# Graph attention on one core: v's first half ahead of the transposes in the prologue, the second spill of row terms moved back, the last maximum turned behind value steps and a second step held

## The reference

```python
h = jnp.maximum(_layernorm(x, axis=-1), 0.0)          # x: 4096 x 256, float32
q, k, v = h @ Wq.T + bq, h @ Wk.T + bk, h @ Wv.T + bv # 256 x 256 weights
a = q @ k.T / 16 + adj + adj                          # 4096 x 4096
x = x + softmax(a, axis=-1) @ v
```

## Time and profile before

| | us |
|---|---|
| median of 3 runs | 810.15 |
| the runs | 810.07, 810.15, 2887.47 |
| the profiled execution | 809.79 |
| its span, first to last instruction | 808.0 |
| TensorE busy in it | 799.6 |
| VectorE, GpSimd, ScalarE busy | 561.3, 412.7, 357.2 |

### The profile page before, as it was taken

One profiled execution on the slowest core, in us unless ns is written; L12 is line 12 of the kernel. 1 busy time (PEld: TensorE's weight loads), 2 busy tenths in 40 slices (PEclk: granted clock), 3 DMA queues, 4 the chain that ended last, 5 costly groups with the idle time before them and its releaser, 6 DMA issues.

```text
span 808.0 us, 16606 instructions
## 1 busy us (share of the span) xinstructions
PE 799.6 (99%) x6652; PEld 797.6 (99%) x6652; DVE 561.3 (69%) x942; ACT 357.2 (44%) x637; POOL 412.7 (51%) x377
## 2 busy tenths in 40 slices
PE   9999999999999999999999999999999999999998
PEld 8999999999999999999999999999999999999998
DVE  6868767676676767667677666767766676776754
ACT  5684434434443443444344444344444444443365
POOL 4545719073471917447091643709164380926573
PEclk9999999999999999999999999999999999999999
DMA  8520434333333334333333333423333343333300
GB/s 256 180 94 5 161 91 120 98 112 97 97 114 93 112 98 110 100 98 119 92 111 93 112 105 91 123 92 106 101 111 106 83 123 91 110 105 94 91 27 14
DMA packets 46398, 83.57 MB, mean 103 GB/s; under 512 B 5616, under 2 KB 8304, under 8 KB 46320
## 3 DMA queue, kind: packets, MB, share of 16 engines
q1 hardware_dynamic: 45744, 81.71, 33.5%
q10 hardware_dynamic: 576, 0.79, 0.3%
HBM read 78.25 MB, written 4.23 MB: 102 GB/s over the span
## 4 chain that ended last, share of the span: by engine, by line
PE 95%; DVE 1%; ACT 1%; POOL 1%; issue 1%; DMA 0%; SPq 0%; POOLq 0%; DVEq 0%
PE ps L393 48%; PE ps L495 15%; PE ps L496 15%; PE ps L497 15%; PE ps L385 1%; PE ps L374 1%; DMA ring_b<-in_adj 0%; ACT x_pair L573 0%; PE ps L404 0%; POOL v L329 0%; DVE x_third L680 0%; POOL rstd L315 0%; SPq L234 0%; DVE ring_b L703 0%; ACT v_full L593 0%
## 5 line engine op out<-in xcount | busy, mean ns | idle before, releaser
L393 PE MATMUL ps<-qhl,hT 128*128 128x256 f32 x3072 | 407.2, 282 | 0.6 <-DVE ring_b L703 0.6
L393 PEld LDWEIGHTS ps<-qhl,hT 128*128 128x128 f32 x3072 | 383.9, 190 | 0.8 <-DVE ring_b L703 0.8
L495 PE MATMUL ps<-v,p_hi 128*128 128x258 f32 x1024 | 290.0, 283 | 0.3 <-DVE p_lo L744 0.3
L496 PE MATMUL ps<-v,p_lo 128*128 128x258 f32 x1024 | 288.8, 282 | 0.0
L497 PE MATMUL ps<-v,p_hi 128*128 128x256 f32 x1024 | 288.4, 282 | 0.0
L640 ACT CAST p_hi<-ps 128x512 fp32r<-128x512 f32 x256 | 150.3, 587 | 264.4 <-PE ps L497 262.6
L364 POOL TENSOR_TENSOR ring_a<-ring_a,m_row 128x512 f32<-128x512 f32 x179 | 226.0, 1300 | 16.3 <-ACT m_row L646 15.6
L703 DVE TENSOR_TENSOR ring_a<-ps,ring_a 128x512 f32<-128x512 f32 x179 | 123.3, 689 | 117.3 <-PE ps L393 116.4
L495 PEld LDWEIGHTS ps<-v,p_hi 128*128 128x128 f32 x1024 | 194.7, 190 | 0.5 <-DVE p_lo L744 0.5
L496 PEld LDWEIGHTS ps<-v,p_lo 128*128 128x128 f32 x1024 | 193.8, 189 | 0.0
L497 PEld LDWEIGHTS ps<-v,p_hi 128*128 128x128 f32 x1024 | 193.2, 189 | 0.0
(11 more groups left out here) (82 smaller groups left out, 340.0 us busy)
## 6 DMA issues: line engine op xcount, KB each, us to landing
ring_a<-in_adj SPq DMA_DIRECT2D x179, 256.0 KB, 2.7
ring_b<-in_adj SPq DMA_DIRECT2D x77, 256.0 KB, 2.7
x_res<-in_x SPq DMA_DIRECT2D x16, 256.0 KB, 3.0
out<-x_res SPq DMA_DIRECT2D x15, 256.0 KB, 2.0
x_pair<-in_x SPq DMA_DIRECT2D x5, 512.0 KB, 4.2
term_row<-term_spill SPq DMA_DIRECT2D x14, 128.0 KB, 3.2
x_third<-in_x SPq DMA_DIRECT2D x2, 512.0 KB, 4.3
w_all<-in_w ACTq DMA_DIRECT2D x3, 256.0 KB, 4.3
```

Of the source, the lines that this page charges most:

```text
L393: last = nc.tensor.matmul(dst, lhs(a, ib), rhs(c, ib), start=(n == 0), stop=(n == 3 * DB - 1))
L495: nc.tensor.matmul(ps[:, at, 0:VW], hi, v[:, n, 0:VW], start=(n == 0), stop=False)
L496: nc.tensor.matmul(ps[:, at, 0:VW], lo, v[:, n, 0:VW], start=False, stop=False)
```

## The change

In the prologue loop on TensorE, `project_v(g, 0)` goes ahead of `transpose_h(g + 2)` and both ahead of `scores(2 * g)`. ScalarE follows with `v_hi(g, 0)` ahead of `h_hi(g + 2)`. On VectorE the low part of h goes behind the adjacency sum, the statistics and the aggregation. q of block 1 moves from iteration 3 to iteration 7. On SyncE `spill_terms(1)` goes from ahead of the last two prologue loads of the ring to behind the load of step 25. In the last block `turn_max` and `spread_max` go behind the value step of their iteration instead of ahead of it, and step 254 is held besides step 251, which makes the loop one iteration longer. For block 0 turn and spread stay where they were.

```diff
-    HOLD = (STEPS - 5,)
+    HOLD = (STEPS - 5, STEPS - 2)
-    Q1_GROUP = 3
+    Q1_GROUP = GROUPS - 1
...
             spill_terms(0)
-            spill_terms(1)
             sp.wait_ge(s_vlo, 2 * GROUPS)
...
+                if s == RING + 2:
+                    spill_terms(1)
...
             for g in range(1, GROUPS):
+                pe.wait_ge(s_hlo, g + 2)
+                project_v(g, 0)
                 if g + 1 < GROUPS:
                     transpose_h(g + 2)
-                pe.wait_ge(s_hlo, g + 2)
-                project_v(g, 0)
-                scores(2 * g)
                 if g == Q1_GROUP:
                     pe.wait_ge(s_vhi, 2 * g)
                     project_q(1)
-                    scores(2 * g + 1)
-                    pe.wait_ge(s_qlo, 2)
-                    project_v(g, 1)
-                elif g + 1 < GROUPS:
+                scores(2 * g)
+                if g + 1 < GROUPS:
                     project_v(g, 1)
                     scores(2 * g + 1)
...
-                if u == 0 and b - 1 in TURNED:
-                    turn_max(b - 1)
-                if u == 1 and b - 1 in TURNED:
-                    spread_max(b - 1)
+                if s == FIRST:
+                    turn_max(0)
+                if s == FIRST + 1:
+                    spread_max(0)
                 if u == UNITS // 2 and b + 1 < BLOCKS:
                     project_q(b + 1)
                 if s not in HOLD and due(s) >= 0:
                     weigh_values(due(s))
+                if s == STEPS:
+                    turn_max(BLOCKS - 1)
+                if s == STEPS + 1:
+                    spread_max(BLOCKS - 1)
...
             for g in range(1, GROUPS):
+                v_hi(g, 0)
                 if g + 1 < GROUPS:
                     h_hi(g + 2)
-                v_hi(g, 0)
                 if g == Q1_GROUP:
                     q_hi(1)
...
             for g in range(1, GROUPS):
-                if g + 1 < GROUPS:
-                    h_lo(g + 2)
                 add_adj(2 * g - 1)
                 if g + XB < GROUPS:
                     for j in range(GT):
                         tile_stats(g + XB, j)
+                    part_stats(g + XB + 1)
+                if g + 1 < GROUPS:
+                    h_lo(g + 2)
                 running_max(2 * g - 1)
-                if g + XB < GROUPS:
-                    part_stats(g + XB + 1)
```

## The result

The changed kernel takes **807.46 us** (median of 9 runs, 807.32 to 807.85), the kernel before 810.08 in the same comparison. The ratio is 0.9969, with a 95% interval of 0.9961 to 0.9977. The forecast was 808.0, in a range of 806.5 to 810.3. The profiled execution took 807.45 us with a span of 805.6; before these were 809.79 and 808.0.

A forecast was written before the change was run, and what follows sets the result against it. TensorE, busy 799.6 of 808.0 us, was taken to bound the kernel, leaving only its waits. Gains of 3.16 us less losses of 1.0 made 2.2 net, so 808.0 us was forecast, range 806.5 to 810.3.

The forecast's parts named there:

- What bounds the kernel: Whole kernel: TensorE is busy 799.6 of 808.0 us, so only its waits, 4.3 us in all, are left to gain.
- Part 1: Prologue, v ahead of the transposes: 1.43 us gained in group 1, 0.42 at ScalarE's normalizing, about 0.5 lost in group 2.
- Part 2: Prologue, q of block 1 moved to the last group: the wait for q's low part goes, 0.57 us gained.
- The tight place: Group 7: scores(16) may start 1.0 us after q's low part and 0.35 after the sum, so no wait.
- Part 3: Second spill behind unit 25's load: the last two ring_b loads come earlier and TensorE's wait goes, 0.74 us gained.
- Part 4: Last block's maximum: the turn's 0.69 us wait goes, a wait of about 0.95 comes behind the spread; costs 0.5.
- The sum: Whole kernel: 3.16 us gained, 1.0 lost, net 2.2; 807.6 from the profiled execution, 808.0 from the median.
- (a): Prologue groups: GpSimd's work on v holds VectorE's maxima and delays h's low part; 811.6 us, chance 0.10.
- (b): Tail: no new wait, because ScalarE's work is further ahead than followed; 806.8 us, chance 0.15.
- (c): Tail: the turn still waits 0.69 us, since the held step does not bring the maximum forward; 808.7 us, chance 0.08.
- (d): Group 1: v(1,0) waits for something too, so the new order does not fill the wait; 809.4 us, chance 0.07.

The follow-up runs named there:

- q_in_group_3: The changed kernel with q of block 1 back in iteration 3, in the old order: 807.97 us, 0.9979 of the kernel before.
- prologue_only: The kernel before with only the prologue's new order and q's new place; spill, turn and hold as before: 807.56 us, ratio 0.9973.
- early_v_lo: The changed kernel with GpSimd's first low part of v ahead of its factors for group 2: 806.05 us, 0.9962 of the kernel before.
- late_copy: The changed kernel with ScalarE's copy of the last spread maximum one step later, behind the next high part: 806.2 us, ratio 0.9959.

## Why the prediction was right

**What bounds the kernel** held: only TensorE's waits could be had, and every term of the sum was one of them.

**Part 1** held in its places and sizes. The transposes stayed bound by the normalizing, 0.48 us late against a forecast of 0.47. The new wait for h's low part came in group 2 and nowhere else, 0.50 from start to start (27.10, against 25.17 + 1.43), forecast 0.5. The groups behind it ran free, as the count of spare time said.

**Part 2** held: no wait for q's low part, and q_in_group_3 gave back 0.72 for the forecast 0.57. The tight place, scores(16), did not wait: it started 0.91 us after q's low part and 0.32 after the sum, forecast 1.0 and 0.35.

**Part 3** held. Forecast 0.74; in the front part of the middle 0.81 in the whole change and 0.84 alone, since the scores behind that wait were slower by 0.1 as well. That the wait can cost 0.47 more behind an earlier prologue, as in the one trace of prologue_only, the prediction did not see. It does not touch the sum of the whole change, where the wait is gone.

**Part 4** held in its mechanism: the turn's wait went, and one for p_lo came at step 235 because one exponential was queued behind the copy. From spread to step it took 2.70 us as forecast. The two small waits for low parts 233 and 234 came as well: those steps start 0.34 and 0.27 behind the transposes ahead of them, and 0.19 and 0.13 in the kernel before. The stage cost 0.60 and not 0.5: step 235 itself lasts 0.1 longer, being the first group after a wait.

**The sum** of the profiled times was 807.6, measured 807.45. That close a match is partly luck. The stages gave -2.16 - 0.47 + 0.60 = -2.03 against the forecast's -2.16, and the trace of the change started 0.35 us earlier than that of before, which no edit did. The terms were mis-sized by 0.24 (prologue, more gained), 0.10 (tail, more lost) and 0.27 (middle: 0.81 gained in front, 0.34 lost to the execution's pace). The forecast priced a wait by the time from start to start and left out that the group behind it is slower. The medians fell by 2.62 and not by 2.2; their interval allows 1.9 to 3.2.

**The rivals.** (a) The running maximum was held by GpSimd, up to 1.36 us for 0.69, so that mechanism is real, but never more than once in a group by more than 0.7, far from the 1.5 spare. The lock that the Trainium skill states (SBUF — State Buffer, "SBUF: two separate sides") is borne out by early_v_lo, in which the normalizing has 0.73 for 2.34, and by the ends of the held maxima (last section). (b), (c) and (d) did not happen: the p_lo wait was there, the turn's was not, and v(1,0) started at once. late_copy makes what (b) supposed, and there the tail is 0.38 under the kernel before and not the 0.69 that (b) priced; the small waits for low parts 233 and 234 stay.

## What to carry to other kernels

When one engine is 99% busy, each wait on it can be priced from start to start and an edit foreseen to a few tenths of a microsecond, if the other engines' queues are followed in order past the wait that goes: here two of the four parts made a new wait, and one of these cost more than it saved. Before an order is moved about to hide a late operation, look why it is late: GpSimd beside VectorE made two normalizings three times as long, and moving one GpSimd instruction gave more than VectorE's order could. And an instruction that waits for another engine's late result (the copy of the maximum) belongs behind everything in its queue that is ready and will be wanted first.

## What the runs showed of the hardware

TensorE's first group after a wait is slower. v's product after one takes 1.55 from start to start (27.10 to 28.65) and 1.43 to 1.44 otherwise (33.82 to 35.26), the eight transposes 0.85 and 0.79. In the tail the first matmul behind a transpose or a wait lasts 0.36 to 0.39 and the others 0.28. In the prologue the kernel before has four such slower groups (0.12 behind q's low part, 0.06 at three transposes: 0.30 together) and the changed one two (0.12 and 0.06: 0.18), so 0.12 of the 0.24 by which the prologue gained more than forecast is explained; the rest is open.

VectorE's low part of h, with one input in PSUM, took 1.19 to 1.23 us everywhere, with GpSimd at work beside it or not. The running maximum with both inputs in SBUF took up to 1.36 in the changed kernel. GpSimd's low parts of v and such maxima in three groups:

```profile
31.94 1.19 POOL L330 TENSOR_TENSOR v<-v_full,v 128x512 fp32r<-128x512 f32 x1
32.33 1.36 DVE L715 TENSOR_TENSOR acc<-acc,ring_a 128x512 f32<-128x512 f32 x1
38.36 1.19 POOL L330 TENSOR_TENSOR v<-v_full,v 128x512 fp32r<-128x512 f32 x1
38.78 1.32 DVE L715 TENSOR_TENSOR acc<-acc,ring_a 128x512 f32<-128x512 f32 x1
44.77 1.19 POOL L330 TENSOR_TENSOR v<-v_full,v 128x512 fp32r<-128x512 f32 x1
45.39 1.12 DVE L715 TENSOR_TENSOR acc<-acc,ring_a 128x512 f32<-128x512 f32 x1
```

The maxima start 0.39, 0.42 and 0.62 after GpSimd's instruction, and each ends 0.55 or 0.56 after its end, whatever it had started with; GpSimd takes 1.19 every time. So all but the first 0.14 of the maximum's 0.69 us came after GpSimd was done: VectorE waited for it, and the two did not share. How long such a maximum takes depends on how much of GpSimd's instruction is still to come.

The same 575 us of TensorE without a single wait varied between executions by up to 0.34 us.
